# Sliding-window attention block on one core: Q and K of the next batch move into the attention loop, and the scores are computed in 64-row halves

## What is computed

```python
xn = _layernorm(x, axis=-1)
q = (x @ Wq + bq).reshape(b, nb, W, H, HD)          # W = 64, H = 16, HD = 16; k and v alike
scores = jnp.einsum('bnqhd,bnkhd->bhnqk', q, kc) * scale      # kc: previous, own and next block
scores = jnp.where(mask[None, None], scores, -1000000000.0)
attn = jax.nn.softmax(scores, axis=-1)
out = jnp.einsum('bhnqk,bnkhd->bnqhd', attn, vc).reshape(b, s, d)
h = layer_norm(out @ Wo + bo + x, g1, b1)
f = jax.nn.gelu(h @ W1 + c1) @ W2 + c2
x = x + layer_norm(f + h, g2, b2) + expert_layer(xn)
```

## Time and profile before

| | |
|---|---|
| median of 3 runs | 1550.31 us (1548.87 to 1557.77) |
| span of the profiled execution | 1553.1 us |
| TensorE, busy share of the span | 80% |
| VectorE | 69% |
| ScalarE | 48% |
| GpSimd | 48% |
| mean granted TensorE clock | 0.913 |

### The profile page before, as it was taken

How to read it: one execution, slowest core, us unless ns; L and a number is a source line. 1 busy time by engine, 2 the same in 40 slices (tenths; PEclk the granted TensorE clock), 3 DMA queues, 4 the chain that set the end, 5 groups by cost and what they waited for, 6 DMA issues and landing times.

```text
span 1553.1 us, 34323 instructions
## 1 busy us (share of the span) xinstructions
PE 1240.9 (80%) x10696; PEld 714.8 (46%) x10696; DVE 1071.5 (69%) x3743; ACT 739.8 (48%) x1356; POOL 739.9 (48%) x749
## 2 busy tenths in 40 slices
PE   0648885999678985999859997689858898599967
PEld 0424452735346353654527454373535535265435
DVE  8656775777757775867757677576766676587565
ACT  1305744366543744447443565426544374445642
POOL 6443745156531766037550474406752177504661
PEclk9959997999989997989979899798988899799979
DMA  7463056220733119130462206422082212912010
GB/s 237 92 139 118 3 117 122 76 92 29 144 79 100 57 69 166 50 112 13 108 131 69 99 8 145 91 83 83 33 156 75 88 57 74 162 48 94 2 28 28
DMA packets 89647, 135.00 MB, mean 87 GB/s; under 512 B 10209, under 2 KB 62305, under 8 KB 87393
## 3 DMA queue, kind: packets, MB, share of 16 engines
...
## 4 chain that ended last, share of the span: by engine, by line
PE 49%; DMA 17%; issue 11%; POOL 8%; DVE 8%; SPq 3%; ACT 3%; DVEq 0%; POOLq 0%; ACTq 0%
DMA pair_dram<-pool 9%; PE bank L1132 8%; PE bank L1035 8%; PE bank L1154 8%; PE bank L1036 7%; PE bank L1038 7%; PE bank L1181 6%; DMA q_s<-q_s 5%; DVE xn L604 2%; SPq L284 2%; DMA ys_dram<-xn 2%; PE bank L1102 2%; POOL x_sb L453 2%; POOL x_sb L451 2%; POOL rs L386 2%
## 5 line engine op out<-in xcount | busy, mean ns | idle before, releaser
L713 DVE CUSTOM_DVE_ANT_0 bank<-bank,mask 128x192 f32<-128x192 f32 x1024 | 337.3, 388 | 199.1 <-PE bank L1132 195.1
L943 ACT ACTIVATE pool<-bank 128x512 f32<-128x512 f32 x512 | 293.0, 597 | 118.9 <-PE bank L1154 113.2
L1132 PE MATMUL bank<-k_s,q_s 128*64 128x192 f16 x2048 | 175.3, 269 | 144.1 <-DMA q_s<-q_s 141.2
L440 POOL TENSOR_SCALAR_AFFINE_SELECT pool<-pool 128x512 f32<-128x512 f32 x256 | 172.2, 675 | 194.1 <-ACT pool L943 193.4
L1154 PE MATMUL bank<-q_s,k_s 128*128 128x256 f16 x1024 | 199.3, 290 | 28.7 <-issue 21.3
L389 POOL TENSOR_TENSOR rs<-ve,neghalf 128x1 f32<-128x1 f32 x64 | 36.9, 577 | 384.8 <-DVE ve L776 384.8
L1132 PEld LDWEIGHTS bank<-k_s,q_s 128*64 128x64 f16 x2048 | 77.8, 113 | 250.1 <-issue 226.9
L1181 PE MATMUL bank<-pool,v_a 128*32 128x256 f32 (+2 forms) x2560 | 161.1, 345 | 19.9 <-DVE pool L727 8.6
L989 ACT ACTIVATE pool<-bank,c1c 128x512 f32<-128x512 f32 x128 | 87.8, 686 | 169.5 <-PE bank L1038 132.5
L790 DVE TENSOR_TENSOR pool<-pool 128x512 f16<-128x512 f32 x128 | 106.7, 839 | 63.3 <-ACT pool L955 62.2
L713 DVE DVE_READ_ACCUMULATOR2_ANT m_sb<- 128x1 f32 x1024 | 144.6, 141 | 0.3
...
## 6 DMA issues: line engine op xcount, KB each, us to landing
...
```

The lines of the kernel that those rows point to most:

```text
L440: nc.gpsimd.affine_select(out=p, in_=p, compare_op=ALU.is_ge, fill=0.0, base=0, pattern=[[0, 4], [1, 2 * W]], channel_multiplier=-1).then_ ...
L713: ins = nc.vector.tensor_tensor_reduce(out=SB[u % 2][:, i * WIN:i * WIN + WIN], in0=SB[u % 2][:, i * WIN:i * WIN + WIN], in1=mask[:, v, :] ...
L943: nc.scalar.activation(prob[:, (k + 2) % 3, 2 * pu:2 * pu + 2, :], TB[u % 2][:, :].rearrange("p (h q) -> p h q", h=2), ACT.Exp, scale=EXP_ ...
L1132: mm = nc.tensor.matmul(SB[u % 2][W * bl:W * bl + W, i * WIN:i * WIN + WIN], q_s[:, h, W + w0:2 * W + w0], k_s[:, h // 2, w0:w0 + WIN], st ...
```

## The change

Three things are changed together.

1. The next batch's work moves forward. Its input is loaded during the W2 stage of the turn before. Its statistics run in steps 0 to 4 of the attention loop (before: step 20), its normalization in steps 8 to 11 (before: 23 to 26), its transposes in steps 11 to 14 (before: 28 to 31), and Q and K in steps 15 to 30, three matmuls a step (before: after b_stage). They use two PSUM banks instead of four. The stores to `pair_dram` and the loads of the stacks are issued from step 18 on; those of the second half of the heads wait until the loop's last transposed scores.
2. The stacks hold two heads on top of each other: rows 0 to 47 and the maximum's row 48 for one, rows 64 to 112 for the other. `q_s` has half the size. A score matmul now uses one 64-row half of the array, and a transposed score matmul too. In steps 1 to 18 the two are issued in turns, the transposed scores on one half and the scores on the other.
3. The band is added by four more matmuls a step (a 64 x 64 identity times a mask), and VectorE takes the maxima of two heads with one plain reduction. `max_cols` uses the score banks `SB` instead of `MB`, so it waits until all issued scores are reduced, and some scores wait for its copy.

```diff
-    XN_AT = 23
+    XN_AT = 8
+    XT_AT = XN_AT + 3
+    QK_AT = XT_AT + 4
+    assert QK_AT + 16 <= STEPS
...
-    pair_dram = nc.dram_tensor("pair_dram", (2, 4, P, S), F16, kind="Internal").ap()
+    pair_dram = nc.dram_tensor("pair_dram", (2, 2, 4, 2, 3, HD, S), F16, kind="Internal").ap()
...
+    MAX_STEPS = [LEAD - T + 3] + [T * g + MAX_AT - 1 + LEAD for g in range(G - 2)]
...
-        mask = sb("mask", [P, 3, WIN], BF16)
+        ident16 = sb("ident16", [P, W], BF16)
+        mask = sb("mask", [P, 3, 2, W], BF16)
...
-        q_s = sb("q_s", [P, H, S + 2 * W], F16)
+        q_s = sb("q_s", [P, H // 2, S + 2 * W], F16)
...
-        QB, VB = TB + MB, OB + TB
+        QB, VB = MB, OB + TB
...
+            def pair_stores(b, i):
+
+                c, qk = divmod(i, 2)
+                for src, done, slots in ((qk_h, qk_hi, (0, 2 if qk else 1)), (qk_l, qk_lo, (1 if qk else 2,))):
+                    sp.wait_ge(done.sem, done.at(b, 2 * i + 2))
+                    for slot in slots:
+                        sp.dma_start(pair_dram[c, qk, :, :, slot, :, :].rearrange("j a d s -> d (j a) s"),
+                                     src[:, 2 * qk + c, :]).then_inc(pair_st[i % 2].sem, 16)
+
+            def stack_loads(b, i, first=False):
+
+                c, qk = divmod(i, 2)
+                if not first and qk == 0:
+                    sp.wait_ge(ST_ps.sem, ST_ps.at(b - 1, 4 * T * (c + 1)))
+                    sp.sem_inc(passed, 1)
+                sp.wait_ge(pair_st[i % 2].sem, pair_st[i % 2].at(b, 48 * (i // 2 + 1)))
+                dst = k_s if qk else q_s
+                for a in range(2):
+                    sp.dma_start(dst[W * a:W * a + KW, 4 * c:4 * c + 4, W:W + S],
+                                 pair_dram[c, qk, :, a, :, :, :].rearrange("j o d s -> (o d) j s")).then_inc(stack[c].sem, 16)
...
+                    if i == 10 and x_next:
+                        load_x(b + 1)
...
-            def turn(b, last):
+            def turn(b, last, x_next=True):
                 max_rows(b, 1)
+                load_res(b)
+                max_rows(b, 2)
                 if not last:
-                    load_x(b + 1)
-                load_res(b)
-                for g in range(2, G):
-                    max_rows(b, g)
+                    pair_stores(b + 1, 0)
+                max_rows(b, 3)
                 if not last:
+                    pair_stores(b + 1, 1)
+                    for i in range(2):
+                        stack_loads(b + 1, i)
+                    for i in range(2, 4):
+                        pair_stores(b + 1, i)
+                    for i in range(2, 4):
+                        stack_loads(b + 1, i)
                     store_res(b + 1)
-                    stacks(b + 1)
-                    sorted_tiles(b + 1)
+                    sorted_tiles(b + 1, x_next)
                 store_out(b)
...
-                    if k == XN_AT - 1 and not last:
+                    if k == TH + 1 and not last:
...
-                for pu in range(2):
-                    u = 2 * j + pu
-                    dve.wait_ge(S_ps.sem, S_ps.at(b, u + 1))
+                for n, par in enumerate((1, 0)):
+                    dve.wait_ge(S_ps.sem, S_ps.at(b, 2 * j + n + 1))
                     dve.sem_inc(passed, 1)
-                    for i in range(2):
-                        h = 4 * g + 2 * pu + i
-                        ins = nc.vector.tensor_tensor_reduce(
-                            out=SB[u % 2][:, i * WIN:i * WIN + WIN], in0=SB[u % 2][:, i * WIN:i * WIN + WIN], in1=mask[:, v, :], scale=1.0,
-                            scalar=-3.0e38, op0=ALU.add, op1=ALU.max, accum_out=m_sb[:, h, t:t + 1])
-                    ins.then_inc(mx.sem, 1)
+                    nc.vector.tensor_reduce(m_sb[:, 4 * g + par:4 * g + 4:2, t],
+                                            SB[par][:, 0:2 * WIN].rearrange("p (h c) -> p h c", h=2), AX.X, ALU.max).then_inc(mx.sem, 1)
...
-                    if k == 2 * T + MAX_AT and not last:
+                    if k < TH and not last:
+                        for t in range(2):
+                            c1_tile(b + 1, 2 * k + t)
+                    if k == TH and not last:
                         c1_stage(b + 1)
                     if k in SHARED:
                         band(b, k)
-                    if XN_AT <= k < XN_AT + T // 2 and not last:
+                    if XN_AT <= k < XN_AT + TH and not last:
                         for t in range(2):
                             xn_tile(b + 1, 2 * (k - XN_AT) + t)
-                    if STEPS - 4 <= k < STEPS and not last:
-                        xn_low(b + 1, k - (STEPS - 4))
+                    if XT_AT <= k < XT_AT + 4 and not last:
+                        xn_low(b + 1, k - XT_AT)
+                    if QK_AT <= k < QK_AT + 16 and (k - QK_AT) % 2 and not last:
+                        qk_low(b + 1, (k - QK_AT) // 2)
...
+            def qk_half(b, u, part):
+
+                o, hf = u % 4 // 2 * 2 + u // 4, u % 2
+                dst = QB[u % 2][:, :]
+                f = slice(o * P, o * P + P)
+                s = slice(hf * HALF, hf * HALF + HALF)
+                if part == 0:
+                    if u >= 2:
+                        pe.wait_ge(qk_lo.sem, qk_lo.at(b, u - 1))
+                    else:
+                        pe.wait_ge(xT_l.sem, xT_l.at(b, 4))
+                    nc.tensor.matmul(dst, wqk_h[:, 0, f], tr_h[:, 0, s], start=True, stop=False)
...
+            def score_mm(out, n, j, par, i):
 
                 g, t = divmod(j, T)
+                h, r = 2 * g + i, slice(W * par, W * par + KW)
+                q = W + (2 * t + n) * W
+                return nc.tensor.matmul(out[W * n:W * n + W, i * WIN:i * WIN + WIN], q_s[r, h, q:q + W], k_s[r, h, q - W:q + 2 * W],
+                                        start=i == 0, stop=False, skip_group_check=True)
+
+            def score_t_mm(out, k, par, i):
+
+                g, t = divmod(k, T)
+                h, r = 2 * g + i, slice(W * par, W * par + W)
+                return nc.tensor.matmul(out[:, i * QW:i * QW + QW], k_s[r, h, W + t * P:W + t * P + P], q_s[r, h, t * P:t * P + QW],
+                                        start=True, stop=True)
+
+            def mask_mm(out, n, t, par):
+
+                r = slice(W * par, W * par + W)
+                band = mask[r, edge(2 * t + n), :, :].unsqueeze(1).broadcast_to([W, 2, 2, W])
+                dst = out[W * n:W * n + W, 0:2 * WIN].rearrange("p (h c k) -> p h c k", h=2, c=3)[:, :, 0::2, :]
+                return nc.tensor.matmul(dst, ident16[r, :], band, start=False, stop=True, skip_group_check=True)
...
+                if j in MAX_STEPS and par == 1:
+                    pe.wait_ge(mT_ev.sem, mT_ev.at(b, MAX_STEPS.index(j) + 1))
+                    pe.sem_inc(passed, 1)
+
+            def scores(b, j, first=False):
+
+                for par in (1, 0):
+                    scores_wait(b, j, par, first)
+                t = j % T
+                for i in range(2):
+                    for n in range(2):
+                        for par in (1, 0):
+                            score_mm(SB[par], n, j, par, i)
+                for n in range(2):
+                    for par in (1, 0):
+                        mm = mask_mm(SB[par], n, t, par)
+                        if n == 1:
+                            mm.then_inc(S_ps.sem, 1)
...
+                j = k - 1 + LEAD
+                both = 1 <= k and j < STEPS
...
+                if both:
+                    scores_wait(b, j, 1 - par)
                 for i in range(2):
+                    mt = score_t_mm(TB[par], k, par, i)
+                    if both:
+                        for n in range(2):
+                            score_mm(SB[1 - par], n, j, 1 - par, i)
+                mt.then_inc(ST_ps.sem, 1)
+                if both:
+                    for n in range(2):
+                        ms = mask_mm(SB[1 - par], n, j % T, 1 - par)
+                    ms.then_inc(S_ps.sem, 1)
...
-                        max_cols(b, k // T + 1)
-                    for pu in range(2):
+                        max_cols(b, k // T + 1, min(k - 1 + LEAD, STEPS))
+                    for par in range(2):
                         if k < STEPS:
-                            scores_t(b, k, pu)
-                        if 1 <= k and k - 1 + LEAD < STEPS:
-                            scores(b, k - 1 + LEAD, half=pu)
-                    if STEPS - 4 <= k < STEPS and not last:
-                        xn_transposes(b + 1, k - (STEPS - 4))
+                            scores_t(b, k, par)
+                    if XT_AT <= k < XT_AT + 4 and not last:
+                        xn_transposes(b + 1, k - XT_AT)
+                    if QK_AT <= k < QK_AT + 16 and not last:
+                        qk_half(b + 1, *divmod(k - QK_AT, 2))
```

203 lines of the change are left out of this document (98 added, 105 removed).

## The result

The changed kernel takes 1845.53 us (median of 4 runs, 1841.99 to 1851.57) against 1552.62 us before in the same comparison: ratio 1.190, interval 1.186 to 1.194. It is 19% slower. I had forecast 1447 us, and the first rival 1559. The profiled execution spans 1840.3 us, 287 more than before, with a mean granted clock of 0.774 instead of 0.913.

The account below looks back on a forecast made before the run. TensorE was taken as nearly always at work, except for gaps in W1 and c2_stage. Middle turns -93 us, last turn -6, prologue -4: -103 from 1553.1 gives a 1450 span, forecast 1447 us, range 1390 to 1575.

Parts of the forecast that it names:

- the first rival: Pairs of steps 1 to 18, all turns: each alternation waits, loop +19.1 us a turn, kernel 1559 us; chance 0.27.
- c2_stage: Stage losing eight Q/K units and a stall, with 7.0 us coming back: from 23.9 to 15.2 us, -8.7 a turn.
- W1: Stage losing the stack wait, with 11 us lost to VectorE behind GpSimd: 35.1 us, -9.9 a turn.
- They run side by side: Steps 1 to 18: wide matmuls on rows 0 to 63 run beside narrow ones on rows 64 to 127; step 1.43 us.
- the other bound: Steps 1 to 18: wide and narrow matmuls wait for each other, four alternations of 0.10 a half; step 2.36 us.
- The rule of the Trainium skill: Pairs of steps 1 to 18: changing tiling mode, not just the tile, drains TensorE; if it holds for half rows, 1559 us.
- the increase that was forecast: Loop: +3.2 us a turn in steps 1 to 18 and +2.1 in steps 19 to 31, together +5.3.
- Steps 19 to 30: Later loop steps, with transposed scores, three Q/K matmuls and values: 1.73 us each, twelve 20.8 instead of 18.6, +2.1 a turn.
- The rival without these stalls: c2_stage and W1: GpSimd's large operations do not hold VectorE, saving 15.7 and 20.9 us; kernel 1321 us; chance 0.08.
- VectorE's reduction: Loop maxima: two reductions of 384 elements a step, each about 0.40 us streaming plus 0.07, instead of four custom operations.
- The last turn's loop: Last turn, 18 steps held at about 1.45 us by GpSimd and ScalarE instead of 1.79: -6 us.
- The transfers: Stack loads delaying residual store, fetch and scatter, W2 10 us late: a rival of 1517 us, chance 0.12; forecast had none late.

Follow-up runs that it names:

- half_grouped: The changed kernel with all four transposed score matmuls of a step first, row halves in turns, then the eight score matmuls and four masks: 1584.7 us, ratio 1.019.
- after_small_adds: The changed kernel with GpSimd's six large operations of a turn on 128 x 8 elements instead of 128 x 2048, leaving out nearly all that work: 1691.4 us, ratio 1.093.
- grouped_pieces: half_grouped with each of GpSimd's six large operations of a turn cut into eight pieces, all work done: 1492.3 us, ratio 0.965.

## Why the prediction was wrong

- **What bounds the kernel** was read rightly as far as c2_stage and W1 go: both waits went, and VectorE beside GpSimd, which replaced them, was forecast.
- **Steps 1 to 18 are where it failed.** The step was "They run side by side", the choice of 1.43 us over 2.36. The runs show the other bound: 2.43 us at full clock. (Its terms as written, 0.52 for the matmuls and 0.40 for the alternations, add up to 0.92 for a half and 2.41 for a step, and not to 0.90 and 2.36; the measured half is 0.93.) I wrote that no row showed the case and then took the kinder value from rows of another case, equal shapes on separate columns. The row that was nearest to unequal shapes was the one I had priced, 0.10 to 0.11 us for every change. The rule of the Trainium skill that I weighed ("TensorEngine Tiling (Array Packing)", Key Properties) was right for halves of rows: both shapes wait, and 1.46 us for half rows against 1.46 for full rows shows it. What it promises for equal modes holds as well: eight narrow matmuls in 0.19 us (911.93 to 912.12 in half_grouped).
- **The clock was in no term.** The rival of 1559 us had the mechanism and was still 287 us short, since it priced the steps from the earlier trace rows, at full clock. Of the 387 us in the loops some 144 are the waiting shapes (1.00 us by 18 steps by 8 turns), 213 the slow clock (1.48 by 18 by 8), and the rest the increase that was forecast. What would have warned me: a loop already at 0.50 when it begins (0.90 is the mean of the loop in the earlier trace rows) has to win the higher clock, and I never asked whether the new order still does.
- **Steps 19 to 30** were forecast at 1.73 us and are 1.65 at full clock (875.68 to 877.33); the twelve take 21.9 us (from 870.60) for the 20.8 of the forecast, as the first of them still runs at 0.50.
- **c2_stage** was forecast at 15.2 us and is 15.5, with the nm of 4.46 us as its cause. **W1** was forecast at 35.1 and is 37.4 in this turn: without the stalls the stage takes 25.8 us and not the 24.1 of my sum, and they cost 11.9 where I had 11. Over seven turns W1 averages 39.2 and gives 6.1 a turn instead of 9.9, and most of that is a larger stall: in three of the seven both products of GpSimd meet two gelu_low in a row (10.25 us together), TensorE waits 8.2 us at once, and W1 is 40 to 42. The rival without these stalls had 8.2 and 24.1 for the two stages; after_small_adds shows 9.8 and 25.8.
- **VectorE's reduction** was forecast at 0.47 us and is 0.56; two in a row take 1.02. **The prologue** gave 3.6 us for 4. **The last turn's loop** costs 38 us more instead of 6 less, by the same failed step.
- **The transfers** were not late in the changed kernel, as I had it. In grouped_pieces TensorE does wait for the sorted tiles, but because GpSimd starts the scatters late and not because of a full queue: with the scatters first, these waits are gone from all turns.
